# Full-size 3x3 convolutions in minimal filtering form along columns, with row parities apart in DRAM, and 7x7 depthwise convolutions as square tiles of TensorE

## The reference, cut to what matters

```python
def _conv(x, w, b, pad, groups=1):
    y = lax.conv_general_dilated(x, w, (1, 1), [(pad, pad), (pad, pad)], ...)
    return y + b[None, :, None, None]

hx = _conv(x, p['conv0_w'], p['conv0_b'], 1)                       # 3x3, 128x128
for l in range(4):
    h = relu(_bn(_block(hx, l, _KS[l], p), ...))                   # sizes 128, 64, 32, 16
    skips.append(h)
    hx = _pool(h)
d = relu(_bn(_block(hx, 4, _KS[4], p), ...))                       # size 8
for i in range(4):
    cat = jnp.concatenate([_up2(d), skips[3 - i]], axis=1)
    d = relu(_bn(_conv(cat, p['dec_w'][i], p['dec_b'][i], 1), ...))  # 3x3, i = 3 is 128x128
return x + _conv(d, p['d0_w'], p['d0_b'], 1)                       # 3x3, 128x128
```

```python
m1 = sigmoid(_conv(x, mask1_w, 1) + mask1_b); m1 = m1 * (m1 >= 0.5); nm1 = _conv(m1, gauss1, 1)
out1 = relu(_bn(_conv(x, conv1_w, 1), ...)) * nm1                  # 3x3, 128x128
out2 = _bn(_conv(out1, conv2_w, 1), ...) * nm2                     # 3x3, 128x128
return relu(out2 + x)
```

## Time and profile before

| what | value |
|---|---|
| device time, median of 3 runs | 8505.98 us (8499.84 to 8510.32) |
| the profiled execution's own time | 8487.06 us |
| its span | 8485.2 us |
| busy: PE, DVE, ACT, POOL | 71%, 60%, 51%, 38% of the span |
| mean granted TensorE clock | 0.902 of full speed |
| five full-size 3x3 convolutions together | 1865 us |
| depthwise at level 1 and at level 2 | 209 us and 130 us |

### The profile page before, as it was taken

One profiled execution on the slowest core, in us unless ns is written; L12 is line 12 of the kernel. 1 busy time (PEld: TensorE's weight loads), 2 busy tenths in 40 slices (PEclk: granted clock), 3 DMA queues, 4 the chain that ended last, 5 costly groups with the idle time before them and its releaser, 6 DMA issues. The chain is left out here.

```text
span 8485.2 us, 82873 instructions
## 1 busy us (share of the span) xinstructions
PE 5984.2 (71%) x26092; PEld 2959.6 (35%) x26286; DVE 5096.2 (60%) x5868; ACT 4346.2 (51%) x4790; POOL 3214.9 (38%) x1140
## 2 busy tenths in 40 slices
...
GB/s 124 131 199 238 59 40 20 40 60 21 40 20 25 65 30 35 192 160 145 24 11 1 105 45 50 42 90 157 103 85 126 149 188 170 188 171 126 181 124 186
DMA packets 1476784, 841.70 MB, mean 99 GB/s; under 512 B 638754, under 2 KB 1406264, under 8 KB 1462664
## 3 DMA queue, kind: packets, MB, share of 16 engines
...
## 5 line engine op out<-in xcount | busy, mean ns | idle before, releaser
L1025 POOL TENSOR_TENSOR ag_D<-ag_X 128x2048 f32<-128x2048 f32 (+15 forms) x940 | 2907.7, 3127 | 1060.9 <-DMA ag_X<-h 941.8
L1089 PE MATMUL ag_slot<-ag_S,ag_w 128*128 128x512 bf16 x4768 | 1470.7, 389 | 838.7 <-DVE ag_J L1131 720.9
L1131 DVE TENSOR_TENSOR ag_J<-ag_J,ag_slot 128x1024 f32<-128x1024 f32 x1240 | 1454.7, 1214 | 153.4 <-PE ag_slot L1089 72.9
L1138 DVE SCALAR_TENSOR_TENSOR ag_J<-ag_slot,ag_J 128x1024 f32<-128x1024 f32 (+14 forms) x1640 | 1436.4, 928 | 0.0
L1056 ACT ACTIVATE ag_slot<-ag_D 128x1024 f32<-128x1024 f32 x1280 | 1308.5, 1025 | 173.8 <-DVE ag_J L1138 58.9
L1040 ACT ACTIVATE ag_A<-ag_D 128x2048 f32<-128x2048 f32 x640 | 1212.1, 1894 | 0.0
L1089 PEld LDWEIGHTS ag_slot<-ag_S,ag_w 128*128 128x128 bf16 x4960 | 286.5, 98 | 2256.7 <-DVE ag_J L1131 1299.8
L1082 PE MATMUL ag_dist<-ag_A,ag_given 128*32 128x512 f32 x5120 | 698.5, 618 | 101.6 <-ACT ag_A L1040 77.6
L255 PE MATMUL dc_ps<-dc_high,dc_w_high 128*128 128x512 f32 (+1 forms) x1056 | 425.2, 403 | 281.2 <-DVE dc_low L68 281.2
L1048 ACT ACTIVATE ag_S<-ag_dist,ag_limit 128x512 bf16<-128x512 f32 x640 | 486.7, 761 | 2.3 <-PE ag_dist L1082 2.3
L269 ACT ACTIVATE dc_out<-dc_ps,shift,scale 128x512 f32<-128x512 f32 (+1 forms) x88 | 67.4, 766 | 818.2 <-PE dc_ps L255 818.2
...
## 6 DMA issues: line engine op xcount, KB each, us to landing
...
wa_x<-r SPq DMA_DIRECT2D x128, 256.0 KB, 2.9
u<-wa_x SPq DMA_DIRECT2D x128, 256.0 KB, 2.4
...
```

The source lines that it names most:

```text
L1025: pool.tensor_tensor(self.tile_part(self.d[u % self.DEPTH][:], u, piece), self.span(g, axis, there, there + hi - lo), self.span(g, axis, l ...
L1089: mm = self.nc.tensor.matmul(self.slot[v % self.SLOTS][:, b, :], self.w[:, weights + 2 * h + b, :], self.s[u % 3][:], start=False, stop=Tr ...
L1131: dve.tensor_tensor(best, best, new, ALU.max).then_inc(self.dve_steps, 1)
L1138: dve.scalar_tensor_tensor(out=best, in0=self.slot_part(v, lo, hi), scalar=-1.0, in1=best, op0=ALU.mult, op1=ALU.max)\
```

## The change: what it does

**`conv_pairs3x3` takes the place of `conv3x3` in the five full-size convolutions.** Along a row, two neighbouring outputs of a 3-tap filter are made from four products in place of six. For inputs d0 to d3, the transformed inputs are d0-d2, d1-d3, d1+d2 and d2-d1; the weights become g0, -g2, (g0+g1+g2)/2 and (g0-g1+g2)/2. The work is cut into 32 units per convolution, 8 row groups of 16 rows times 4 images, written out without loops. In a unit and source, POOL makes the four transformed inputs by three instructions (576, 576 and 1152 elements, both inputs in the slab, stride 2), ACT rounds all 2304 elements to `high`, DVE subtracts for `low` (2304), and PE does 24 matmuls of 512 columns, the two middle products first, then the two edge products: 768 per convolution, 1536 for dc3. ACT brings the middle products to SBUF (1024), DVE makes their sum and difference (2 x 512) and adds the edge products from PSUM (1024), ACT applies scale and bias (1024), and DVE multiplies and adds as before, on 1024 elements at a time; the clip in c2 goes to ACT. All transfers are issued by SP. `split` steers POOL (its transform may be two units ahead of `low`, one in dc3), and `combined`, `evacuated` steer PE's four accumulators.

The diff, cut to its core:

```diff
+            for t in n.by_parity:
+                for p in range(PAIRS):
+                    for parity, row in ((0, 0), (1, t.shape[3] - 1)):
+                        sp.dma_start(t[p, :, parity, row, :], zero[0:P, 0:t.shape[4]]).then_inc(stored, 16)
                         count += 1
...
+def conv_pairs3x3(nc, name, srcs, weights, dst, pad, size, func, scale, bias, mul=None, add=None, relu_after=False):
...
+    units = [(i, m) for i in range(H // (2 * half)) for m in range(IMG)]
+    NU = len(units)
+    LEAD = 2 if ns == 1 else 1
+    SLABS, DIFFS, SPLITS, OUT = LEAD + 1, LEAD, LEAD + 1, 3
...
+        if len(t.shape) == 5:
+            return t[p, m * C:(m + 1) * C, r % 2, at:at + count, :]
+        return t[p, m * C:(m + 1) * C].rearrange("c (t e) w -> c e t w", e=2)[:, r % 2, at:at + count, :]
...
+        slab = [ring(f"slab{s}_", SLABS, [P, half + 1, W + 2]) for s in range(ns)]
+        diff = [ring(f"diff{s}_", DIFFS, [P, 4, half + 1, J]) for s in range(ns)]
+        high = [ring(f"high{s}_", SPLITS, [P, 4, half + 1, J], F32R) for s in range(ns)]
+        low = [ring(f"low{s}_", SPLITS, [P, 4, half + 1, J], F32R) for s in range(ns)]
...
+            def load(u):
+                reach(sp, transformed, 3 * ns * (u - SLABS + 1))
+                for s in range(ns):
+                    for e in range(2):
+                        sp.dma_start(slab[s][u % SLABS][e * C:(e + 1) * C], of_parity(srcs[s], 0, u, e, half + 1))\
+                          .then_inc(slab_loaded[u % SLABS], 16)
...
+            def store(u):
+                sp.wait_ge(finished, u + 1)
+                for e in range(2):
+                    sp.dma_start(of_parity(dst, pad, u, e, half), out[u % OUT][e * C:(e + 1) * C]).then_inc(stored[u % OUT], 16)
...
+            for u in range(NU + 3):
+                if there(u + SLABS):
+                    load(u + SLABS)
+                if extra and there(u):
+                    load_extra(u)
+                if there(u - 3):
+                    store(u - 3)
...
+        def _(pool):
+            for k in range(OUT):
+                pool.memset(out[k][:], 0.0).then_inc(zeroed, 1)
+            for u in range(NU):
+                pool.wait_ge(slab_loaded[u % SLABS], 32 * ns * (u // SLABS + 1))
+                for s in range(ns):
+                    if u >= DIFFS:
+                        pool.wait_ge(split, ns * (u - DIFFS) + s + 1)
+                    by_parity = slab[s][u % SLABS][:].rearrange("c r (j e) -> c e r j", e=2)
+                    d = diff[s][u % DIFFS]
+                    pool.tensor_tensor(d[:, 2], by_parity[:, 1, :, 0:J], by_parity[:, 0, :, 1:J + 1], ALU.add).then_inc(transformed, 1)
+                    pool.tensor_tensor(d[:, 3], by_parity[:, 0, :, 1:J + 1], by_parity[:, 1, :, 0:J], ALU.subtract)\
+                        .then_inc(transformed, 1)
+                    pool.tensor_tensor(d[:, 0:2], by_parity[:, :, :, 0:J], by_parity[:, :, :, 1:J + 1], ALU.subtract)\
+                        .then_inc(transformed, 1)
...
+            def products(u, k, bank):
+                for s in range(ns):
+                    for a in range(2):
+                        for c, (wt, rows_in) in enumerate(((g_high, high[s][u % SPLITS]), (g_high, low[s][u % SPLITS]),
+                                                           (g_low, high[s][u % SPLITS]))):
+                            mm = nc.tensor.matmul(bank, wt[:, k, 2 * s + a, :], rows_in[:, k, a:a + half, :],
+                                                  start=(s == a == c == 0), stop=(s == ns - 1 and a == 1 and c == 2))
+                return mm
...
+            for u in range(NU):
+                pe.wait_ge(split, ns * (u + 1))
+                reach(pe, evacuated, u - 1)
+                for b, k in enumerate(MIDDLE):
+                    mm = products(u, k, middle[u % 2][:, b])
+                mm.then_inc(summed, 1)
+                reach(pe, combined, u - 1)
+                for b, k in enumerate(EDGES):
+                    mm = products(u, k, edges[u % 2][:, b])
+                mm.then_inc(summed, 1)
...
+            def round_high(u):
+                reach(act, summed, 2 * (u - SPLITS + 1))
+                for s in range(ns):
+                    act.wait_ge(transformed, 3 * (ns * u + s + 1))
+                    act.activation(high[s][u % SPLITS][:], diff[s][u % DIFFS][:], ACT.Copy).then_inc(rounded, 1)
+            def evacuate(u):
+                act.wait_ge(summed, 2 * u + 1)
+                reach(act, halved, 2 * (u - 1))
+                act.activation(mid[u % 2][:], middle[u % 2][:], ACT.Copy).then_inc(evacuated, 1)
+            def affine(u):
+                act.wait_ge(combined, u + 1)
+                reach(act, stored[u % OUT], 32 * (u // OUT))
+                act.activation(inside(u).rearrange("c r (j e) -> c r j e", e=2),
+                               both[u % 2][:].rearrange("c e r j -> c r j e"), func, bias=bias, scale=scale).then_inc(scaled, 1)
...
+            def low_part(u):
+                reach(dve, summed, 2 * (u - SPLITS + 1))
+                for s in range(ns):
+                    dve.wait_ge(rounded, ns * u + s + 1)
+                    split_low(dve, low[s][u % SPLITS][:], diff[s][u % DIFFS][:], high[s][u % SPLITS][:]).then_inc(split, 1)
+            def halve(u):
+                dve.wait_ge(evacuated, u + 1)
+                reach(dve, scaled, u - 1)
+                dve.tensor_tensor(both[u % 2][:, 0], mid[u % 2][:, 0], mid[u % 2][:, 1], ALU.add).then_inc(halved, 1)
+                dve.tensor_tensor(both[u % 2][:, 1], mid[u % 2][:, 0], mid[u % 2][:, 1], ALU.subtract).then_inc(halved, 1)
+            def combine(u):
+                dve.wait_ge(summed, 2 * u + 2)
+                dve.wait_ge(halved, 2 * u + 2)
+                dve.tensor_tensor(both[u % 2][:], both[u % 2][:], edges[u % 2][:], ALU.add).then_inc(combined, 1)
+            def finish(u):
+                dve.wait_ge(scaled, u + 1)
+                dve.wait_ge(extra_loaded[u % OUT], extra * (u // OUT + 1))
+                if mul is not None:
+                    dve.tensor_tensor(inside(u), inside(u), mult[u % OUT][:], ALU.mult).then_inc(multiplied, 1)
+                if mul is not None and add is not None:
+                    dve.wait_ge(multiplied, u + 1)
+                if add is not None:
+                    dve.tensor_tensor(inside(u), inside(u), plus[u % OUT][:, :, 1:W + 1], ALU.add).then_inc(added, 1)
...
+            for u in range(NU + 2):
+                if there(u - 1):
+                    combine(u - 1)
+                if extra and there(u - 2):
+                    finish(u - 2)
+                if there(u + LEAD):
+                    low_part(u + LEAD)
+                if there(u):
+                    halve(u)
...
+def cpe_tiles(nc, name, src, bands, dst, size):
...
+    KS = C // NG
+    BATCH = 4
+    KB = KS // BATCH
+    RING = 8 // NG
...
+            for t in range(BATCH):
+                for g in range(NG):
+                    at = slice(g * KS + t * KB, g * KS + (t + 1) * KB)
+                    sp.dma_start(band[rows(g), t * KB:(t + 1) * KB], bands[:, at, :, :]).then_inc(loaded[t], 16)
+                    for m in range(IMG):
+                        sp.dma_start(x[rows(g), t * KB:(t + 1) * KB, m, :], s_v[3:R + 3, at, m, :]).then_inc(loaded[t], 16)
+            for t in range(BATCH):
...
+            for k in range(KS):
+                if k % KB == 0:
+                    pe.wait_ge(loaded[k // KB], per_batch)
+                reach(pe, added, (k - RING + 1) * NG)
+                for dw in range(7):
+                    for g in range(NG):
+                        mm = nc.tensor.matmul(of_step(k, g), band[rows(g), k, dw, :], x[rows(g), k, :, dw:dw + W],
+                                              start=(dw == 0), stop=(dw == 6))
+                mm.then_inc(summed, 1)
...
+                        act.dma_start(of_parity[p, :, e, bass.ds(i0 * rows, rows), :],
+                                      out[p][:].rearrange("c (r w) -> c r w", w=side)).then_inc(stored[p], 16)
...
-                    sp.dma_start(gated[k, p].rearrange("m h w -> h m w"), nm[:, p, 2 * k:2 * k + 2, :]).then_inc(stored, 16)
+                    for e in range(2):
+                        sp.dma_start(gated[k, p, :, e].rearrange("m t w -> t m w"), nm[e:P:2, p, 2 * k:2 * k + 2, :]).then_inc(stored, 16)
...
+    dec.append(dram("dec3", [PAIRS, P, 2, S0 // 2 + 1, S0 + 2]))
+    r0 = dram("r0", [PAIRS, P, 2, S0 // 2 + 1, S0 + 2])
+    gated = dram("gated", [2, PAIRS, 2, 2, S0 // 2, S0])
+    r1a = dram("r1a", [PAIRS, P, 2, S0 // 2 + 1, S0 + 2])
...
-        conv3x3(nc, "conv0", [a.x], a.conv0_w, hx[0], 3, S0, ACT.Identity, 1.0, raw("conv0_b"))
+        conv_pairs3x3(nc, "conv0", [a.x], a.conv0_w, hx[0], 3, S0, ACT.Identity, 1.0, raw("conv0_b"))
...
+            elif l < 3:
+                cpe_tiles(nc, f"cpe{l}_", hx[l], a.band[l], cpe[l], SIZE[l])
...
```

(25 more changed lines are left out.)

180 lines of the change are left out of this document (146 added, 34 removed).

## The result

The changed kernel takes **8230.27 us** (median of 4 runs, 8221.46 to 8239.27) against 8506.99 before, a ratio of 0.9673 (95% interval 0.9657 to 0.9688): 277 us faster where 136 were forecast. Its profiled execution took 8239.27 us.

A forecast was written before the change was run, and what follows sets the result against it. PE's matmuls were taken to bound the five convolutions. Convolutions -7, depthwise level 1 -79, level 2 -55, masks +5 sum to -136 us: 8506 becomes 8370. The forecast's own range was 8270 to 8480, the full range 7850 to 8660.

The forecast's parts named there:

- The mechanism: Convolutions: POOL's transforms and DVE's instructions with two SBUF inputs take turns; 1858 us against 1865, minus 7; chance 0.37.
- POOL's price: Three transforms per convolution unit and source: 2.10 ns per element, 0.20 us fixed; 4.84 us streaming, 5.44 in all.
- the prediction's last line: Wrong at the root if POOL's strided instructions cost something other than 2.1 ns per element, or unrolled queues wait for code.
- My rule: Convolutions: in POOL's and DVE's turns only streaming excludes, fixed parts pass beside it; 8.31 us per conv0 unit.
- Rival 1: Convolutions: POOL and DVE run side by side; 1357 us, minus 508, kernel 7870 us; chance 0.22.
- Rival 2: Convolutions: POOL and DVE take turns by whole instructions; 2075 us, plus 210, kernel 8587 us; chance 0.27.
- Rival 3: Convolutions: PE waits a third of each unit and its clock falls to 1.2 GHz; kernel 8646 us; chance 0.06.
- Rival 4: Depthwise levels: places of PE's array don't run at once; level 1 takes 233 us, kernel 8513, no change; chance 0.08.
- Level 1: Depthwise stage: 209 us become 130, minus 79, with bands loaded once and two places of PE's array at once.
- level 2: Depthwise stage: 130 us, minus 55; SP's queue of 80 loads and 64 stores takes over at 0.48 us per issue.
- Masks: Mask stages: four more stores and taps in runs of 520 bytes; plus 5 us, between 0 and 20.

The follow-up runs named there:

- the probe: Changed kernel plus a measuring stage behind its end: POOL subtractions (1152 elements) beside DVE's (2304, both inputs in SBUF); a pair every 4.40 us, POOL's eight 25.9 us.

## Why the prediction was wrong

- **The mechanism held; a term of the sum was mis-sized.** The step that failed is POOL's price, "2.10 ns per element and 0.20 us fixed", taken from the earlier trace rows. Those instructions read two inputs that lie apart. The convolutions' read neighbours in one slab: 1.15 us for 576 elements and 2.13 for 1152, 1.70 ns per element, three in 4.3 us where I put 4.84 of streaming and 5.44 in all. On the streaming that is 0.92 us for each of 192 units and sources, 177 us. "That the new ones read with stride 2 is in no row; I take the same price": that price had no row of this form behind it, and the range gave a cheaper POOL and a shorter level 2 only some 100 us together, though the prediction's last line names just this as the way to be wrong at the root.
- **A smaller error pulled the other way.** My rule was that only the streaming excludes. With 1.70 ns per element it gives 3.92 + 2.40 + 1.07 = 7.39 us for conv0's unit and 1858 - 177 = 1681 for the five stages; 7.69 and 1725 were measured, so 44 of the 177 us were lost again. In the probe the rule comes within 1%: a pair takes 4.40 us, the streams are 1.96 + 2.40 = 4.36, the whole durations 2.12 + 2.55 = 4.67. In conv0 the whole durations give 4.43 + 2.56 + 1.39 = 8.38. Of conv0's 0.30 us above the rule, 0.17 went with one more buffer: a wait that I had put at nothing. How the rest, and the other stages' share, splits up is open. With a POOL price near the forecast's the kernel took 8437 us, 67 above the forecast, dc3 562 in place of 538: turns and waits beyond my rule cost there too.
- **Rival 1** (side by side) is out by the probe. **Rival 2** (whole instructions) is out by the probe's 4.40 against 4.67; its 8587 failed by the same price as well. **Rival 3**: the mean granted clock was 0.82 to 0.92 of full speed in four of five stages, where it had been 0.91 to 0.97, but PE waits for DVE there and is not the bound. **Rival 4** is out: level 1's 448 matmuls of 256 columns took 99 us of PE, not 206.
- **Level 1** 128 us (130), **level 2** 78 (75): pairs of places at once (99 / 224 = 0.44 us a pair) and SP's 0.48 us per issue (64 stores in 31.6 us) were right. **Masks** cost 10 us in place of 5: from its first load to the first load of `masks`, `mask_taps` went from 93 to 104 us with stores into every other row, and ACT there now waits 37 us for those stores.
